# First attention of a two-layer transformer kernel: centring and scaling of the tiles of x on GpSimd instead of VectorE

## The reference

```
mod = (silu(c) @ wmod)                       # shift sa, scale ca, gate ga, ...
h = layernorm(x) * (1 + ca) + sa             # layernorm: (x - mean) / sqrt(var + eps)
q, k, v = h @ wq.T + bq, h @ wk.T + bk, h @ wv.T + bv      # 32 heads of 16
scores = einsum('bshd,bstd->bsht', q, k) / 4 # within one token, head against head
context = einsum('bsht,bstd->bshd', softmax(scores), v)
x = x + ga * context
```

## Time and profile before

| | us |
|---|---|
| median of 3 runs | 1062.76 |
| lowest and highest | 1059.85, 1064.47 |
| the profiled execution | 1062.04 |
| its span in the profile | 1060.2 |
| busy in it: TensorE, VectorE, ScalarE, GpSimd | 870.1, 772.3, 530.1, 522.7 |

### The profile page before, as it was taken

One profiled execution on the slowest core, in us unless ns is written; L12 is line 12 of the kernel. 1 busy time (PEld: TensorE's weight loads), 2 busy tenths in 40 slices (PEclk: granted clock), 3 DMA queues, 4 the chain that ended last, 5 costly groups with the idle time before them and its releaser, 6 DMA issues. The chain is left out here.

```text
span 1060.2 us, 15006 instructions
## 1 busy us (share of the span) xinstructions
PE 870.1 (82%) x4504; PEld 556.7 (53%) x4504; DVE 772.3 (73%) x1583; ACT 530.1 (50%) x1142; POOL 522.7 (49%) x449
## 2 busy tenths in 40 slices
PE   7488884799977955899998989997989898985477
PEld 1367763666666733455545555554455555553145
DVE  0669997734545535798999899999899999984353
ACT  1377773622214724455555555654555565553143
POOL 2043332011120006678778877885878877873003
PEclk9789987699998977699999999998999999999679
DMA  9420000800005760445555555553555555555101
GB/s 330 163 102 2 2 2 1 288 1 1 1 9 218 259 169 3 115 115 122 125 120 124 125 122 123 122 127 92 118 123 123 126 124 122 125 127 132 55 10 70
DMA packets 73105, 112.29 MB, mean 106 GB/s; under 512 B 18816, under 2 KB 23936, under 8 KB 72768
## 3 DMA queue, kind: packets, MB, share of 16 engines
q1 hardware_dynamic: 60736, 94.54, 32.3%
q10 hardware_dynamic: 12288, 16.79, 6.6%
HBM read 42.06 MB, written 2.10 MB: 42 GB/s over the span
## 5 line engine op out<-in xcount | busy, mean ns | idle before, releaser
L1334 DVE TENSOR_REDUCE nmax<-bank 128x1 f32<-128x512 f32 x256 | 173.9, 679 | 55.6 <-PE bank L1274 53.5
L1409 ACT ACTIVATE prob<-bank,nmax 128x512 f32<-128x512 f32 x172 | 118.5, 689 | 171.1 <-DVE nmax L1334 171.1
L1468 POOL TENSOR_TENSOR prob<-prob,rinv 128x512 f32<-128x512 f32 x129 | 133.7, 1044 | 51.7 <-DVE rinv L1341 51.7
L1349 DVE STREAM_TRANSPOSE blk<-prob 128x512 f32<-128x512 f32 x172 | 120.8, 703 | 3.1 <-ACT prob L1424 0.4
L1272 PE MATMUL bank<-xk_hi,q_hi 128*128 128x512 f32 x256 | 110.5, 432 | 14.7 <-ACT prob L1409 11.7
L1463 POOL TENSOR_TENSOR q_lo<-stage_a,q_hi 128x512 fp32r<-128x512 f32 x64 | 82.3, 1286 | 54.1 <-ACT q_hi L1403 54.1
L1273 PE MATMUL bank<-xk_lo,q_hi 128*128 128x512 f32 x256 | 103.0, 402 | 0.0
L1274 PE MATMUL bank<-xk_hi,q_lo 128*128 128x512 f32 x256 | 101.8, 398 | 0.0
L1409 ACT ACTIVATE stage_a<-bank,nmax 128x512 f32<-128x512 f32 x84 | 57.9, 689 | 75.5 <-DVE nmax L1334 75.5
L1272 PEld LDWEIGHTS bank<-xk_hi,q_hi 128*128 128x128 f32 x256 | 49.1, 192 | 78.7 <-issue 34.0
L1459 POOL TENSOR_TENSOR stage_a<-stage_a 128x512 f32<-128x512 f32 x64 | 82.8, 1293 | 6.3 <-DVE stage_a L1329 6.3
(11 more groups left out here) (214 smaller groups left out, 2155.5 us busy)
## 6 DMA issues: line engine op xcount, KB each, us to landing
pT<-blk SPq DMA_DIRECT2D x384, 64.0 KB, 2.0
raw_e<-blk SPq DMA_DIRECT2D x384, 64.0 KB, 2.0
wmod<-in_wmod SPq DMA_DIRECT2D x12, 1024.0 KB, 11.9
raw_e<-in_wo SPq DMA_DIRECT2D x8, 1024.0 KB, 6.3
pT<-blk ACTq DMA_DIRECT2D x128, 64.0 KB, 2.2
raw_e<-blk ACTq DMA_DIRECT2D x128, 64.0 KB, 2.1
wqn<-in_wqn SPq DMA_DIRECT2D x8, 512.0 KB, 4.0
stage_a<-in_wqkv SPq DMA_DIRECT2D x4, 768.0 KB, 8.9
```

What stands on the lines that cost most here:

```text
L1334: dve.tensor_reduce(nmax[:, s % RING:s % RING + 1], s_bank[s % 2][:, :], AX.X, ALU.max, negate=True).then_inc(max_done, 1)
L1349: dve.transpose(blk[:, u % T_SLOTS, :, :, 32 * st:32 * st + 32].rearrange("p j k q -> p k j q"), prob[s % RING]).then_inc(blk_done, 1)
L1409: act.activation(prob[s % RING], s_bank[s % 2][:, :], ACT.Exp, bias=nmax[:, s % RING:s % RING + 1], accum_out=rsum[:, s % RING:s % RING + ...
L1468: pool.tensor_tensor(prob[s % RING], prob[s % RING], bc(rinv[:, s % RING:s % RING + 1], [P, S]), ALU.mult).then_inc(norm_pool, 1)
```

## The change

`dve_xn` of tile 0 stays on VectorE. Tile 1's moves to the front of GpSimd's queue, behind two waits, for `rstd` and for tile 0's `xn`. Tile t+2's moves from VectorE's step t, where it stood between the V turn and the finish, to the end of GpSimd's step t, behind the residual sum of tile t-1. The operation and its wait on `xT` are the same.

```diff
--- before.py
+++ after.py
@@ -474,6 +474,9 @@
                         pool.tensor_tensor(hv_lo[:, t % 2, :, :, :], by_four(nrm.f), hv_hi[:, t % 2, :, :, :].bitcast(F32),
                                            ALU.subtract).then_inc(hv_lo_done, 1)
 
+                    pool.wait_ge(nrm.rstd, 1)
+                    pool.wait_ge(nrm.xn, 1)
+                    nrm.dve_xn(pool, 1)
                     h_rest(0)
                     hv_rest(0)
                     pool.memset(vT[:, :, :], 1.0).then_inc(pad_set, 1)
@@ -491,6 +494,8 @@
                                                ALU.mult).then_inc(og_done, 1)
                             pool.wait_ge(og_done, t)
                             pool.tensor_tensor(x[:, t - 1, :], x[:, t - 1, :], o_g[:, :], ALU.add).then_inc(x1_done, 1)
+                        if t + 2 < TILES:
+                            nrm.dve_xn(pool, t + 2)
 
                 @block.scalar
                 def _(act):
@@ -543,7 +548,6 @@
                 @block.vector
                 def _(dve):
                     nrm.dve_xn(dve, 0)
-                    nrm.dve_xn(dve, 1)
                     dve.wait_ge(bias_in, 16)
 
                     def k_turn(t):
@@ -636,8 +640,6 @@
                         if t < TILES:
                             q_turn(t)
                             v_turn(t)
-                        if t + 2 < TILES:
-                            nrm.dve_xn(dve, t + 2)
                         if t >= 1:
                             finish(t - 1)
                         if t >= 2:
```

## The result

The changed kernel takes 1073.39 us (median of 4 runs, 1071.41 to 1076.82) against 1063.62 for the kernel before (4 runs): ratio 1.0101, 95% interval 1.0068 to 1.0134. Timed again in another session with more runs, the ratio was 1.010 (1.0082 to 1.0118). It is slower by about 10 us. I had forecast 1062.5 with a range up to 1066.3. The profiled execution took 1073.77 us, its span is 1072.0, which is 11.8 more than before.

What follows compares the result with a forecast made beforehand. VectorE sets the pace in steps 1, 2 and 4, late projections slow 3 and 5; changes of -0.42 + 0.55 - 0.01 - 0.42 + 0.04 + 0 = -0.26 us give 1061.8, and 0.7 for the median gives 1062.5, range 1059.0 to 1066.3.

Steps and rivals of the forecast that it cites:

- 0.42 us of pace for each n_x taken off VectorE: VectorE's queue, first attention: tiles 3 to 7 each save 0.42 us of pace, 2.1 us if nothing else is late.
- Tiles 1 and 2 cost nothing: GpSimd at the start and in step 0: both moved n_x fit where nobody waits, so cost nothing and gain nothing.
- The ring, step = x + 13.20: Loop o_tok, GpSimd, TensorE, V sum, o_tok: a step lasts at least x + 13.20, x being GpSimd's n_x; 14.24 us forecast.
- T: Start of VectorE's o_tok turn in the first attention, from which times within a step are counted.
- x = 1.04 us, with 0.53 and 1.59 as the ends: Assumed GpSimd n_x time: 1.04 from a broadcast-column product, 0.53 from a fill, 1.59 from a difference with a strided operand.
- The case with 2.58: Within the rival "GpSimd is dear": n_x takes two passes of 1.29 us, steps 15.78, sum +5.5 us, 1068.2; chance 0.09.
- 3x - 3.4: Sum over the first attention's steps with the clock as it was: total change in us, a cost from x = 1.13 on.
- The clock as it was: TensorE's granted clock in the five steps stays unchanged; with x from 0.8 to 1.6 this is the forecast case, chance 0.47.
- the slow clock stretches vanish: Rival: TensorE's pause splits, clock stays high, steps 3 and 5 take 14.24; sum -2.35 us, 1060.4; chance 0.2.
- GpSimd is dear: Rival: n_x on GpSimd between residual sum and transposes is slow, x = 2.58, sum +5.5 us, 1068.2; chance 0.09.
- More slow stretches: Rival: split TensorE pauses bring the 5th step's low clock to steps 1, 2 and 4; +4.7 us, 1067.5; chance 0.09.
- 769 ns for a tight loop of 512 elements: Skill's GpSimd price for a one-input loop, cited for a lower n_x cost: sum -1.1 us in place of -0.3.

Runs made afterwards that it cites:

- the better place: Changed kernel with GpSimd's n_x of tile t+2 ahead of its wait for o_tok instead of behind the residual sum: 1061.61 us, ratio 0.9986; again 1060.68 us, 0.9974.
- x = 1.04: Changed kernel with GpSimd's n_x of tiles 2 to 7 cut to one product with a broadcast column, centring left out: 1062.39 us, ratio 0.9988.
- the pause filled: Changed kernel with eight more matmuls, results overwritten, on TensorE ahead of the transposes of tiles 3 to 7: 1065.57 us, ratio 1.003.
- the old loop: Kernel before, profiled as it was (1062.04 us), with ten GpSimd operations added in the first stage (1064.91 us), and with only tile 1's n_x on GpSimd (1063.22 us).

## Why the prediction was wrong

By its own steps:

- *0.42 us of pace for each n_x taken off VectorE*: right for the steps. 13.69 became 13.27 and 14.25 became 13.83 where nothing else was late (n_x in the better place). The 0.42 that the sum takes off ahead of the first turn did not show: from the stage's start to it took 33.15 us before, 33.16 and 33.31 in the better place.
- *Tiles 1 and 2 cost nothing*: right, for tile 1 by its own run; GpSimd's n_x of tile 1 takes 2.08 us in a gap of 3.4. For tile 2 no run tested it alone.
- *The ring, step = x + 13.20*: right. 14.24 at x = 1.04, 15.3 at x = 2.07, in the ten unstretched steps of the changed kernel's profiles and in the five steps with the pause filled. VectorE waits at the Q sum rather than the V sum: at x = 2.07 the Q sum comes at T+9.37 and the V sum 2.80 later, which is within 0.1 us of when V ends, so the two were a tie.
- *x = 1.04 us, with 0.53 and 1.59 as the ends*: this step failed. Measured: 2.07, outside the bounds. I took the price of a product with a broadcast column for that of a two-operation scalar form, because both stream one tile, and I let the highest row I had (a two-input form) stand for a ceiling, though none of the rows had two arithmetic operations. The case with 2.58, "one pass per operation", was the nearer one and got 0.09. With x = 2.07 my own sum gives steps of 15.27 four times and 15.90 once, so -0.42 + 1.58 + 1.02 + 0.18 + 1.07 + 0 = +3.4 us, 1066.2, which is just inside the range. The shorthand in the prediction, 3x - 3.4, would give 2.8; it leaves out that the third step grows too once x + 13.20 is above 14.67.
- *The clock as it was*: this step failed too, and against the kernel before as it was it is the larger one. The prediction had the low clock as two rivals, and took for the bad one 3 x 1.66 us on top of x = 1.04. Measured: 1.6 us a stretched step, in two, four or five steps, so 3.1 us in the first profile and, with 15 stretched steps in five profiles, 3 x 1.6 = 4.8 in the mean. That 1.66 comes so near is luck: it was the distance from a ring step of 14.24 to an old step of 15.90, which was itself 2.0 longer than at full clock (13.88). The clock did not stay as it was for the assumed x either: with x = 1.04 both old low-clock steps were gone, as in the rival "the slow clock stretches vanish" (-2.35 us in its sum, 2.0 less in the stage).
- The two failures are not independent, and I treated them as if they were. A longer x is a longer pause: 1.1 us of waiting before the transposes on the mean for x = 1.04, with no low clock in any of the five steps profiled, 1.8 to 3.3 for x = 2.07, with low clock in 15 of 25 steps. The Trainium skill has the pattern, in "TensorE: Matmul & The Clock Gate", section "HAM oscillation — how this bites in real kernels": waits between bursts of matmuls let the clock fall back, and each burst then begins slow. The Trainium skill has it there for waits on a DMA, and behind every wait. This trace agrees in the pattern (0.63 us a matmul behind the pause, 0.40 before it), and so does the run with filled pauses. It differs in that the waits here were for GpSimd and only 15 of 25 brought it. The pattern should have raised the chance of the case.
- *Rivals*: "GpSimd is dear" had the right mechanism and the right place; that it costs from x = 1.13 on was not tested, the runs have 1.04 and 2.07 only. "More slow stretches" came true beside it. By the sums of the steps, ring 3.4 and clock 4.7 give the stage's 8.0 us to within 0.1. Of the 10 us of the total, about 2 lie outside the stage and stay unexplained.
- The prediction cited the Trainium skill for a lower price: GPSIMD Engine Reference, "Elementwise — side-by-side cycle accounting", 769 ns for a tight loop of 512 elements. Its best case does not hold for this operation: a copy takes 0.61 us, the scalar forms 1.49 to 2.07.

## What to carry to other kernels

An operation moved to an idle engine is free only if it stands where that engine idles: behind a wait that hangs on the bottleneck's last result it joins the ring, ahead of that wait it costs nothing. Price it by a row with the same form and the same number of arithmetic operations, and where there is none keep a multiple of the nearest row in the range, not beside it. When a move makes TensorE wait, count the matmuls behind the wait at the lower clock as well: here that was 4.7 us on the mean, 2.4 of which the kernel before paid already in another place, and it differed from execution to execution. Filling the pauses of both kernels is what told the two parts apart.

## What the runs showed of the hardware

- GpSimd at 128x512 float32: two operations with per-partition operands 2.07 us, one 1.56, two with constants 1.93, one 1.49, product or difference with a broadcast column 1.04, product of two tiles 1.26, copy 0.61. VectorE does the first in 0.51 to 0.55.
- GpSimd's n_x took 2.06 to 2.10 us at every place, beside VectorE's turns and softmax or with VectorE idle.
- Useless matmuls in a pause made the stage shorter: 141.0 to 137.4 us in the changed kernel, 134.7 to 132.8 in the kernel before.
- Once a step of the changed kernel fell under the low clock, all later ones of the five did, in five executions of five; where it began differed, behind pauses of 1.87 to 2.53 us, while pauses of 1.84 to 2.57 us in other steps brought no low clock. With the old loop it was the 3rd and the 5th step that were stretched, in three executions of three.
